# Two graph convolutions: 24 edge tiles fetched by GpSimd instead of row by row from two queues

## What is computed

```python
def gcn_conv(x, edge_index, W, b):
    ...
    row = jnp.concatenate([edge_index[0], loop])
    col = jnp.concatenate([edge_index[1], loop])
    ...
    norm = deg_inv_sqrt[row] * deg_inv_sqrt[col]
    h = x @ W
    msg = h[row] * norm[:, None]
    out = jax.ops.segment_sum(msg, col, num_segments=n)
    return out + b
...
h = gcn_conv(x, edge_index, W1, b1)
h = gcn_conv(h, edge_index, W2, b2)
return jax.nn.leaky_relu(h, negative_slope=0.1)
```

## Time and profile before

| what | us |
|---|---|
| median of 3 executions (8212.72 to 8237.21) | 8221.33 |
| the profiled execution, its own time | 8201.55 |
| its span | 8199.4 |
| TensorE busy | 4673.6 (57%) |
| GpSimd busy | 4097.0 (50%) |
| VectorE busy | 3858.8 (47%) |
| ScalarE busy | 2384.3 (29%) |

### The profile page before, as it was taken

How to read it: one execution, slowest core, us unless ns; L and a number is a source line. 1 busy time by engine, 2 the same in 40 slices (tenths; PEclk the granted TensorE clock), 3 DMA queues, 4 the chain that set the end, 5 groups by cost and what they waited for, 6 DMA issues and landing times. The chain is left out here.

```text
span 8199.4 us, 115932 instructions
## 1 busy us (share of the span) xinstructions
PE 4673.6 (57%) x26878; PEld 3753.7 (46%) x27040; DVE 3858.8 (47%) x13515; ACT 2384.3 (29%) x5196; POOL 4097.0 (50%) x4201
## 2 busy tenths in 40 slices
PE   3444444545555566664666665556666645666666
PEld 2444444435555555662333333333333335565566
DVE  4555555554444447973333333333333334454445
ACT  3444444333333336860000000100000024444443
POOL 2555555435665655435544454545544434555552
PEclk7676667656666667996888888788888865555556
DMA  4444444214444445531111111111111112222221
GB/s 134 113 115 116 114 114 116 73 53 119 123 122 122 124 126 157 186 119 44 41 39 38 40 41 32 53 35 41 41 40 40 38 45 38 44 43 43 43 44 35
DMA packets 751490, 624.11 MB, mean 76 GB/s; under 512 B 350006, under 2 KB 645002, under 8 KB 750858
## 3 DMA queue, kind: packets, MB, share of 16 engines
q0 software_dynamic: 153856, 344.32, 16.2%
q1 hardware_dynamic: 587164, 270.42, 12.3%
q10 hardware_dynamic: 9840, 2.68, 0.1%
HBM read 532.42 MB, written 84.51 MB: 75 GB/s over the span
## 5 line engine op out<-in xcount | busy, mean ns | idle before, releaser
L1218 POOL DMA_INDIRECT sum_rows<-tab_row,src_idx x1480 | 1424.6, 963 | 1534.8 <-PE sum_pA L1298 737.0
L1266 PE MATMUL sum_pX<-sum_mask,sum_part 128*128 128x512 bf16 x4836 | 1240.1, 403 | 326.5 <-issue 293.5
L1367 DVE TENSOR_TENSOR acc<-acc,sum_pA 128x128 f32 x1664 | 479.1, 288 | 1693.9 <-PE sum_pA L1298 942.7
L631 POOL DMA_INDIRECT l_rows<-tab_qv,src_idx x832 | 794.2, 955 | 766.4 <-DVE l_wrow L849 433.9
L631 POOL DMA_INDIRECT l_rows<-tab_wh,src_idx x832 | 787.2, 946 | 725.2 <-DVE l_wrow L849 392.9
L366 POOL DMA_INDIRECT l_rows<-tab_ax,src_idx x832 | 803.3, 965 | 549.4 <-issue 249.1
L653 PE MATMUL l_pK<-l_winr,l_hotT 128*128 128x128 f32 (+1 forms) x3328 | 707.7, 355 | 464.3 <-issue 355.4
L1266 PEld LDWEIGHTS sum_pX<-sum_mask,sum_part 128*128 128x128 bf16 x4998 | 499.7, 103 | 951.7 <-issue 504.4
L653 PEld LDWEIGHTS l_pK<-l_winr,l_hotT 128*128 128x128 f32 x3328 | 666.5, 297 | 498.4 <-issue 380.3
L681 PE MATMUL l_pA<-l_hotA,l_wrow 128*128 128x128 f32 x3328 | 761.7, 396 | 96.8 <-issue 67.7
L681 PEld LDWEIGHTS l_pA<-l_hotA,l_wrow 128*128 128x128 f32 x3328 | 684.5, 299 | 108.9 <-issue 96.5
(11 more groups left out here) (276 smaller groups left out, 7844.2 us busy)
## 6 DMA issues: line engine op xcount, KB each, us to landing
l_winr<-tab_k SPq DMA_DIRECT2D x832, 64.0 KB
spill<-l_rows SPq DMA_DIRECT2D x104, 512.0 KB
sum_rows<-spill SPq DMA_DIRECT2D x104, 512.0 KB
sum_rows_r<-tab_row SPq DMA_DIRECT2D x3072, 0.5 KB
sum_rows_r<-tab_row ACTq DMA_DIRECT2D x3072, 0.5 KB
l_winr<-tab_b SPq DMA_DIRECT2D x840, 32.0 KB
sum_line<-src_lo SPq DMA_DIRECT2D x104, 256.0 KB
sum_rows<-tab_row,src_idx POOLq DMA_INDIRECT x1480
```

What stands on the lines that cost most here:

```text
L631: nc.gpsimd.indirect_dma_start(rows[:, g % R, u, :], None, table, bass.IndirectOffsetOnAxis(src_idx[:, t:t + 1], 0)).then_inc(s_rows[g % R ...
L1218: nc.gpsimd.indirect_dma_start(rows[:, g % R, u, :], None, tab_row, bass.IndirectOffsetOnAxis(src_idx[:, t:t + 1], 0)).then_inc(s_rows[g % ...
L1266: last = nc.tensor.matmul(pX[:, k % 2, :], part[:, i, h, :], mask[:, step % MASKS, :], start=h == 0 and i == 0, stop=h == NB - 1 and i == 2)
L1367: nc.vector.tensor_tensor(acc[:, bass.ds(at, P)], acc[:, bass.ds(at, P)], pA[:, q % HOTS, u, :], ALU.add).then_inc(s_add, 1)
```

## The change

There are no r groups any more. Their six groups become f groups, so that there are 191 f groups and 17 x groups. GpSimd issues 764 gathers per convolution instead of 740. The buffer `rows_r`, the list `line`, their semaphores, `rows_one_by_one` and the waits on them are gone. ScalarE's queue in the loop holds only `take` and `take_turned`. SyncE's holds only the loads `lines(k)`, each of which waits as before for the code of k - 1 (`s_code`), but is no longer tied to a place among row DMAs. The 833 steps are spread over 174 f groups instead of 168, about 4.79 per f group instead of 4.96. The total of matmuls, masks, one-hots and adds is the same.

```diff
-            XG, RG = 17, 6
-            NF = NG - XG - RG
+            XG = 17
+            NF = NG - XG
...
-                order += [("r", j) for j in range(RG) if (j + 1) * 29 == g]
...
-                def rows_one_by_one(q, half, c):
...
-                    if j >= 2 and c % (CHUNKS // RG) == 0:
-                        q.wait_ge(s_sum, place["r", j - 2] + 1)
...
-                    for i in range(LOAD):
-                        q.dma_start(rows_r[p0 + i:p0 + i + 1, j % 2, u, :], tab_row[bass.ds(of[i], 1), :]
-                                    ).then_inc(s_r[j], 16)
...
                         lines(0)
-                        sp.dma_start(line[:], bass.AP(tensor=a["src_run"].tensor, offset=R0, ap=[[RE, 1], [1, RE]])
-                                     ).then_inc(s_line, 16)
-                        sp.wait_ge(s_line, 16)
-                        done = 0
-                        for g in range(NF):
-                            for k in range(1, XG):
-                                if (whole[k - 2] if k >= 2 else 0) + 3 == g:
-                                    lines(k)
-                            for c in range(done, min(CHUNKS, chunk_at(g + 1))):
-                                rows_one_by_one(sp, 0, c)
...
+                        for k in range(1, XG):
+                            lines(k)
...
                                 take_turned(whole.index(g - 4))
-                            for c in range(done, min(CHUNKS, chunk_at(g + 1))):
-                                rows_one_by_one(ae, G // 2, c)
-                            done = min(CHUNKS, chunk_at(g + 1))
...
-                            elif kind == "x":
+                            else:
                                 pe.wait_ge(s_x, g + 1)
                                 of = rows_x[:, g % 2]
-                            else:
-                                pe.wait_ge(s_r[g], 16 * P * G)
-                                of = rows_r[:, g % 2]
```

More of the change, by code:

```diff
@@ L1102, in convolve @@
             NG = T // G
-            XG, RG = 17, 6
-            NF = NG - XG - RG
+            XG = 17
+            NF = NG - XG
             XS, MASKS, AHEAD = XG * NB, 16, 2
-            X0, R0 = NF * G * P, (NF + XG) * G * P
-            RE = RG * G * P
+            X0 = NF * G * P
             def steps_until(g):
@@ L1115, in convolve @@
             whole = [next(g for g in range(NF) if steps_until(g) >= (k + 1) * NB) for k in range(XG)]
-            CHUNKS = RG * (G // 2) * P // LOAD
-            def chunk_at(g):
-                return g * CHUNKS // (NF - 8)
             order = []
@@ L1130, in first_tile @@
                 kind, g = order[q]
-                return (g + {"f": 0, "x": NF, "r": NF + XG}[kind]) * G
+                return (g + {"f": 0, "x": NF}[kind]) * G
             with Phase(nc) as cx:
@@ L1137, in convolve @@
                 rows_x = sb(L + "rows_x", [P, 2, G, F], fp32, cx)
-                rows_r = sb(L + "rows_r", [P, 2, G, F], fp32, cx)
                 turned = sb(L + "turned", [P, G * P], fp32, cx)
@@ L1146, in convolve @@
                 p_of = sb(L + "p_of", [P, 1], fp32, cx)
-                line = sb(L + "line", [1, RE], i32, cx)
                 pA = ps(cx, L + "pA", [P, HOTS, G, P])
@@ L1167, in convolve @@
                 s_third = sem(cx, L + "s_third")
-                s_line = sem(cx, L + "s_line")
-                s_r = [sem(cx, L + f"s_r{j}") for j in range(RG)]
-                def rows_one_by_one(q, half, c):
-                    u, p0 = half + c // (P // LOAD) % (G // 2), c % (P // LOAD) * LOAD
-                    j = c // (P // LOAD) // (G // 2)
-                    if j >= 2 and c % (CHUNKS // RG) == 0:
-                        q.wait_ge(s_sum, place["r", j - 2] + 1)
[L1177 to L1180, removed]
-                    for i in range(LOAD):
-                        q.dma_start(rows_r[p0 + i:p0 + i + 1, j % 2, u, :], tab_row[bass.ds(of[i], 1), :]
-                                    ).then_inc(s_r[j], 16)
                 with nc.Block() as block:
@@ L1196, in _ @@
                         lines(0)
-                        sp.dma_start(line[:], bass.AP(tensor=a["src_run"].tensor, offset=R0, ap=[[RE, 1], [1, RE]])
-                                     ).then_inc(s_line, 16)
-                        sp.wait_ge(s_line, 16)
-                        done = 0
-                        for g in range(NF):
-                            for k in range(1, XG):
-                                if (whole[k - 2] if k >= 2 else 0) + 3 == g:
-                                    lines(k)
-                            for c in range(done, min(CHUNKS, chunk_at(g + 1))):
-                                rows_one_by_one(sp, 0, c)
-                            done = min(CHUNKS, chunk_at(g + 1))
-                        for j in range(RG):
-                            sp.wait_ge(s_r[j], 16 * P * G)
+                        for k in range(1, XG):
+                            lines(k)
                     @block.gpsimd
@@ L1243, in _ @@
                             nc.scalar.activation(part[:, 1, i * GB:(i + 1) * GB, :], rest[:], ACT.Copy).then_inc(s_second, 1)
-                        ae.wait_ge(s_line, 16)
-                        done = 0
                         for g in range(NF):
```

## The result

The changed kernel takes 7662.64 us (median of 4, 7644.03 to 7674.8), the kernel before 8220.27 (8212.72 to 8237.21): a ratio of 0.9321, 95% interval 0.9303 to 0.9339, or 558 us less. The forecast was 7791 us, 430 less. The profiled execution has a span of 7654.5 us against 8199.4.

The account below looks back on a forecast made before the run. The prediction took the row queues as the bound, with GpSimd's gathers next: 102 + 1077 + 22 = 1201 us per convolution, 430 less in all, so 7769 us of span and 7791 us median; range 7370 to 7900.

Parts of the forecast that it names:

- The bound before: Both convolutions: no engine's work bounds them; the row queues set the pace, with twelve TensorE waits, 497.1 us.
- 24 gathers more: GpSimd, each convolution: added gathers lie on the path, 37 us per convolution, 74 in all; convolution rebuilt as 1201 us.
- the 1.55 us per gather: GpSimd's traced pace, between 1.46 and 1.58, applied to 695 gathers per convolution: 1077 us.
- The other two terms: Start and end of each convolution: 69 gathers in the first 102 us, and 22 us for sums after the last gather.
- The last steps of the forecast: From 7769 us of span: 2.2 us around it, then 19.8 us from profiled execution to median, giving 7791 us.
- The first rival: GpSimd's pause behind each group shrinks or goes with the row DMAs: 7375 to 7665 us; chance 0.18.
- the main case: The rebuilt sum holds, with gathers at 1.46 to 1.58 us and the rule's 26 us: 7665 to 7870; chance 0.65.
- Its signs: Trace if right: no row issue, 764 gathers at 1.5 to 1.6 us, pauses near 1.4, convolutions near 1200, clock above 0.9.
- The rival's full form: GpSimd without the pause: 1.25 us per gather, a convolution of 993 us, 7375 us in all.
- x groups as the pace: TensorE waits up to 9.73 us for each of 34 x groups, losing 330 us: 7870 to 8121; chance 0.11.
- The third rival: TensorE's clock stays at the lower level, 8.8 us per group: up to 8795 us; chance 0.06, shared with slower gathers.
- The rule against GpSimd: VectorE holding the shared port would make each added gather cost 2.10 us: 26 us more in the total.

Follow-up runs that it names:

- the mark: The changed kernel itself, unaltered, timed once more beside the kernel before on another chip: 7593.54 us, ratio 0.9343.

## Why the prediction was right, and where its size was off

*The bound before.* Right as far as it went: twelve waits, 497.1 us, and the row queues as the pace. But the waits hid a second lateness that the prediction did not cost: SyncE's loads behind the row DMAs. "SyncE's loads come earlier; nothing is queued behind their wait" looked at the wrong side, since the loads themselves had been queued behind rows. The run without the twelve waits shows it: with two thirds of the rows still brought it is 259 us faster, not 539, and VectorE waits 376.8 us for the loads. This did not spoil the sum, because it was not made from the waits, but rebuilt from GpSimd's pace in stretches that hold neither a wait for r rows nor one for these loads.

*24 gathers more.* Right in kind: GpSimd's gathers are the pace in the changed kernel. The term that was mis-sized is the 1.55 us per gather. Measured are 1.47, and 695 x 0.08 = 56 us per convolution, 112 in both, are nearly all of the 128 us between 7791 and 7663. The other two terms came out at 71 gathers in the first 102 us (69 forecast) and 16 us for the tail (22, so 12 in both). The last steps of the forecast were off too, and in part cancel: the median lies 6.4 us above the profiled execution and not 19.8, and the rest of the span grew by 7 us.

*Why 1.47.* The prediction took the pause of 1.4 us behind each group as given and let it go only as a rival, with "it is rather the gathers that hold the row queues up". Both are true: gathers slow the queues, and rows in the queues cost the gathers something. SyncE's rows alone, with the loads out of their way, cost 0.015 to 0.02 us per gather, about a quarter of the distance to 1.55. With both queues bringing rows, and the intervals of 10 us and more left out, a group takes 6.03 us (f groups 18 to 129), against 5.82 in the mark and 6.09 in the kernel before, counted from GpSimd's timelines. That is 0.21 of 0.27, about three quarters, though on three chips and with a limit of 10 us that was chosen: with 12 us the run with both queues reaches the 6.13 of the kernel before. So the row DMAs beside the gathers make most of the difference; whether the restarts after each wait add to it is open.

*The first rival* (the pause shrinks or goes, 7375 to 7665 us) has happened in part. Every second pause is gone, those left are longer, and the time beyond 1.25 us per gather fell from 0.30 to 0.22, about a quarter. The measured 7663 lies 2 us inside this rival's stretch and not in that of the main case (7665 to 7870). So the range held, but the case that the prediction gave 0.65 did not come out as it stood. Its signs say the same: no row issue, 764 gathers and no gap of 40 us are as written; 1.47 us per gather (1.5 to 1.6), pauses of 1.96 us behind every second group (1.4 throughout) and convolutions of 1140 us (1200) are not. The rival's full form, 1.25 us per gather, did not come when the wait was replaced: the run in which GpSimd didn't wait for sums is the slowest of all.

*x groups as the pace:* no gap ended by `sum_rows_x` is left in TensorE's list. *Clock:* 0.88 and 0.89 over the convolutions, where the prediction wrote above 0.9, and 0.92 in their middle; before it was 0.81. The third rival, a lower clock that makes it slower, did not come.

*Two slips* that change nothing: the "15 steps" beside an f group are 15 matmuls of five steps, and the pace at which nothing would be gained is (1418 - 102 - 22) / 695 = 1.86 us per gather, not 1.83.

*The rule against GpSimd.* The gathers of the middle last 656.93 / 692 = 0.949 us each, no longer than in the earlier trace rows, so VectorE did not hold them up beside its masks. The Trainium skill, page "SBUF — State Buffer", section "A bandwidth-pool intuition that's wrong (but worth ruling out)", says that GpSimd can't write descriptors until VectorE releases the port that both share. In the middle of the convolutions this trace shows no such delay. What GpSimd's gathers do to the other engines, which the run without pauses shows, is the opposite direction, and cost more.

## What to carry to other kernels

When a queue is overfull, the named wait is only the first thing it delays: undo the wait alone, and see what else stands behind the same instructions. Size a change from stretches in which none of the removed waits acts, but remember that the removed work was still running beside them; most of the 0.08 us per gather went unseen there. And don't take away a wait of GpSimd's gathers because GpSimd looks idle in it: here that wait was what the other engines ran in.

## What the runs showed of the hardware that was not expected

- A stream of indirect DMAs from GpSimd without pauses (691 in 946 us, 1.37 us each) slowed TensorE's plain matmuls to 2.1 to 2.8 us apart, let VectorE have one sum in about 60 us, and left the granted clock at 0.52. With the stream over, the same matmuls ran at a clock of 1.00, 3600 in 637 us. In which part of the chip the two meet, no run shows.
- The pause of GpSimd is mostly longer behind more gathers, as medians 1.4 us behind four and 2.3 behind eight in the kernel before, 2.0 behind eight in the changed kernel, and 1.9 behind eight and 2.6 behind twelve in the mark. Without the steps there is no such order (2.9 behind 24, 3.7 behind 20). A deeper ring or more masks don't change the mean, 1.46 to 1.48 us per gather, and leaving out three quarters of TensorE's matmuls took 67 us off both convolutions together.
- Row DMAs of 512 bytes took 1.07 us each beside gathers without longer gaps (121 in 129.26 us, SyncE, with the loads at ScalarE), 62 to 66 us per 80 (0.8 each) where the gathers had gaps, and 0.56 each in a stretch in which TensorE and GpSimd mostly stood.
